# Cross-attention added to a batch: plain fp32 queries and keys, probabilities transposed in place, and the first row tile added by whole rows

## What is computed

```python
x, ctx: (32, 512, 512) fp32;  Wq, Wk, Wv: (512, 512) fp32;  16 heads of 32
q = (x @ Wq.T)  k = (ctx @ Wk.T)  v = (ctx @ Wv.T)      # split into heads
probs = softmax(q k^T / sqrt(32));  att = probs v
return x + att[0]          # the attention of batch 0, added to every batch
```

## Time and profile before

| | |
|---|---|
| median of 3 executions | 189.42 us (188.5 to 189.72) |
| the profiled execution | 188.74 us, span of its instructions 186.6 us |
| PE, DVE, ACT, POOL busy | 127.9, 105.7, 96.3, 80.7 us |
| moved by DMA | 71.52 MB, mean 383 GB/s |
| DMA issues of 256 KB, 512 KB, 1 MB | 32, 48, 32 and a few at the start |

### The profile page before, as it was taken

The page is one execution under the profiler, slowest core; times in us unless marked ns, Lnnn a source line. Parts: engine busy times, 40 slices in busy tenths (PEclk is TensorE's granted clock), DMA queues, the critical chain, the costliest instruction groups (busy, mean ns, idle before and its releaser), DMA issues.

```text
span 186.6 us, 3382 instructions
## 1 busy us (share of the span) xinstructions
PE 127.9 (69%) x1240; PEld 94.0 (50%) x1240; DVE 105.7 (57%) x171; ACT 96.3 (52%) x225; POOL 80.7 (43%) x45
## 2 busy tenths in 40 slices
PE   6999999999995978998889998798881000000000
PEld 6878877668663756775657666565550000000000
DVE  0455646643709999636699766945618999300000
ACT  2525535566476789679698778898860000000000
POOL 1000000000009999800099996399966999200000
PEclk9999999999999999999999999999999555555555
DMA  6999999999998999999999999999999999999996
GB/s 211 378 359 418 410 409 410 408 407 407 383 410 293 331 332 344 343 305 382 395 386 398 386 367 404 403 407 404 406 416 416 408 422 421 412 418 421 421 421 258
DMA packets 31968, 71.52 MB, mean 383 GB/s; under 512 B 1872, under 2 KB 10064, under 8 KB 31824
## 3 DMA queue, kind: packets, MB, share of 16 engines
q1 hardware_dynamic: 31952, 71.31, 99.9%
HBM read 37.75 MB, written 33.55 MB: 382 GB/s over the span
## 4 chain that ended last, share of the span: by engine, by line
PE 52%; DVE 14%; ACT 13%; issue 6%; DVEq 1%; POOL 0%; ACTq 0%; POOLq 0%
PE bank L387 12%; PE bank L367 8%; ACT probs L586 7%; PE bank L322 6%; PE bank L356 6%; PE bank L345 6%; DVE slots L719 5%; ACT probs_t L594 5%; PE bank L314 5%; PE bank L398 4%; DVE slots L709 3%; DVE neg_max L666 3%; PE bank L469 3%; DVE slots L702 1%; PE bank L409 1%
## 5 line engine op out<-in xcount | busy, mean ns | idle before, releaser
L272 POOL TENSOR_TENSOR slots<-slots,att_rows 128x512 f32<-128x512 f32 (+1 forms) x27 | 43.4, 1650 | 70.0 <-DVE att_rows L691 70.0
L586 ACT ACTIVATE probs<-bank,neg_max 128x512 f32<-128x512 f32 x64 | 44.9, 702 | 12.1 <-DVE neg_max L666 11.7
L666 DVE TENSOR_REDUCE neg_max<-bank 128x1 f32<-128x512 f32 x64 | 41.8, 682 | 11.9 <-PE bank L367 11.8
L387 PE MATMUL bank<-ident,probs 128*128 128x128 f32 x256 | 39.8, 281 | 7.8 <-ACT probs L586 6.7
L594 ACT COPY probs_t<-bank 128x512 f32<-128x512 f32 x64 | 37.7, 592 | 10.8 <-PE bank L387 10.0
L387 PEld LDWEIGHTS bank<-ident,probs 128*128 128x128 f32 x256 | 28.1, 140 | 21.3 <-ACT probs L586 17.1
L367 PE MATMUL bank<-k_t,x_q 32*128 32x512 f32 x192 | 24.1, 425 | 0.0
L278 POOL TENSOR_TENSOR slots<-slots,att_rows 128x1024 f32<-128x1024 f32 x8 | 18.6, 2377 | 4.8 <-DVE att_rows L691 4.8
L286 POOL TENSOR_TENSOR slots<-slots,att_rows 128x2048 f32<-128x2048 f32 x4 | 18.0, 4532 | 3.4 <-DVE att_rows L691 3.4
L702 DVE TENSOR_TENSOR slots<-slots,bank 128x512 f32<-128x512 f32 (+1 forms) x21 | 17.7, 856 | 0.1
L398 PE MATMUL bank<-probs_t,v 128*32 128x128 f32 x512 | 17.3, 276 | 0.7 <-ACT probs_t L594 0.7
(11 more groups left out here) (41 smaller groups left out, 98.6 us busy)
## 6 DMA issues: line engine op xcount, KB each, us to landing
slots<-in_x_dram SPq DMA_DIRECT2D x19, 1024.0 KB, 14.5
slots<-in_x_dram SPq DMA_DIRECT2D x26, 512.0 KB, 8.6
...
```

Of the source, the lines that this page charges most:

```text
L272: nc.gpsimd.tensor_tensor(xs, xs, a.unsqueeze(1).to_broadcast([P, BPS, a.shape[1]]), ALU.add).then_inc(added[g], 1)
L387: last = nc.tensor.transpose(bank[:, PT_BANK + h % 2, t * P:(t + 1) * P], probs[:, h % 2, t * P:(t + 1) * P], ident[:, :])
L586: nc.scalar.activation(probs[:, h % 2, :], bank[:, h % S_BANKS, :], ACT.Exp, bias=neg_max[:, h:h + 1], scale=1.0, accum_out=row_sum[:, h:h ...
L666: nc.vector.tensor_reduce(neg_max[:, h:h + 1], bank[:, h % S_BANKS, :], AX_X, ALU.max, negate=True).then_inc(max_ready, 1)
```

## The change

- Keys, queries, query weights and transposed x are plain fp32 in one piece; a query chunk and a head's scores are one matmul each. Weights of keys and values and the context stay split. Transposed x lies in the place of the raw queries, and there is one `q_t`.
- After the weights, ACT no longer empties banks: x0_t, q and q_t of row tiles 1 to 3 are copied by DVE. In `heads` of PE, turn 11 and score pair 7 go ahead of `turn_queries`.
- The probabilities of a head stay in one place: ACT writes them there, PE transposes them out of it, ACT copies the transposed ones back over it. Heads 0 to 3 of row tile 0 have places of their own in slot 15's memory, all later ones share a ring of 7. `exponent` waits until the head that had the place 7 heads ago has been weighed; it no longer waits for a transposition.
- 20 slots: groups 0 to 3 of the last half (`FRESH`) are loaded at the start. The load of slot 15 waits for the first weighing. Only groups 4 to 9 are reloaded row by row, 10 to 15 whole.
- Row tile 0 is turned back, normalised, added and stored as whole rows after all 16 heads. Three of the value chunks and the queries of row tile 1 stand later in PE's order.

The diff, without hunks that only rename units or follow from these:

```diff
@@ -29,12 +29,12 @@
     C = D // P
     HG = HEADS // HPG
     GROUPS = B // BPS
-    SLOTS = GROUPS + 1
+    SLOTS = GROUPS + 4
     PAIR = 2
     PAIRS = HEADS // PAIR
     S_BANKS = 4
     PT_BANK, BACK_BANK, ATT_T_BANK = 4, 6, 7
-    PT_SLOTS = 6
+    RING = 7
     WARM_UP = 24
     SCALE = float(DK) ** -0.5
     HI, LO = 0, 1
...
-    FIRST, SECOND, ROW_1, ROW_2, ROW_3 = 1, 2, 3, 4, 5
-    BY_ROWS, ADDED_BY_ROWS, STORED_BY_ROWS = 12, (1, 2, 3, 4, 5, 6, 7, 8), (1, 2, 3)
-    LAST_ROW_DVE_GROUPS = (4, 5, 6, 7, 8, 1, 2, 3)
...
-    FIRST_ORDER = (0, 1, 3, 2, 5, 7, 4, 9, 6, 8, 11, 10, 13, 12, 14, 15)
+    ROW_0, ROW_1, ROW_2, ROW_3 = 1, 2, 3, 4
...
+    FRESH = SLOTS - GROUPS
+    BY_ROWS = range(FRESH, FRESH + 6)
+    ADDED_BY_ROWS, STORED_BY_ROWS = (0, 1, 2, 3, 4, 5, 6, 7), (0, 1, 2)
...
...
+    FIRST_ORDER = (0, 1, 2, 3, 4, 5, 7, 6, 9, 8, 11, 10, 13, 12, 14, 15)
...
-        WQ_RAW, WK_RAW, CTX_RAW, WV_RAW, WK_T, CTX_T, WV_T = 7, 8, 9, 10, 11, 13, 15
...
+        WQ_RAW, WK_RAW, CTX_RAW, WV_RAW, WK_T, FIRST_PROBS, CTX_T, WV_T = 10, 11, 12, 13, 14, 15, 16, 18
...
-        BY_ACT = [what != "v" for what, *_ in JOBS]
-        BY_DVE = [what != "q" for what, *_ in JOBS]
+        SPLIT = ("wk_t", "ctx_t", "wv_t")
+        BY_ACT = [n <= number["wv_t", C - 1] for n in range(len(JOBS))]
+        BY_DVE = [what in SPLIT or not BY_ACT[n] for n, (what, *_) in enumerate(JOBS)]
...
         def slot_of(J, g):
-            return g if J == 0 else (g - 1) % SLOTS
...
+            return (J * GROUPS + g) % SLOTS
...
+        def place(j, h):
+            n = j * HEADS + h
+            return first_probs[:, n, :] if n < HPG else ring[:, (n - HPG) % RING, :]
+        def place_free(eng, j, h):
+            last = j * HEADS + h - RING
+            if last >= HPG:
+                eng.wait_ge(att_t_summed, last // HPG + 1)
...
-                    load(0, g)
-            sp.wait_ge(half_values_done, 1)
-            load(0, CTX_T)
-            load(0, WV_T)
+                if g == FIRST_PROBS:
+                    sp.wait_ge(att_t_summed, 1)
+                load(0, g)
             sp.wait_ge(bank_filled, number["v", T - 1] + 1)
-            load(0, CTX_T + 1)
-            load(LAST_HALF, 0)
-            LAG = 3
-            for g in FIRST_ORDER:
-                store(FIRST, g)
-            for g in range(GROUPS):
-                store(SECOND, g)
-            for g in range(1, BY_ROWS + 1):
-                reload_row(0, g)
+            for g in range(FRESH):
+                load(LAST_HALF, g)
+            LAG, ROW_LAG = 3, 10
+            for n, g in enumerate(FIRST_ORDER):
+                store(ROW_0, g)
+                if n >= ROW_LAG:
+                    reload_row(0, BY_ROWS[n - ROW_LAG])
             for g in range(GROUPS):
                 store(ROW_1, g)
-                if g >= LAG:
-                    reload(g - LAG + 1)
-            for g in range(GROUPS - LAG + 1, GROUPS):
-                reload(g)
+                if LAG - 1 <= g < GROUPS - FRESH + LAG - 1:
+                    reload(g - LAG + 1 + FRESH)
...
                     emptied(pe, "x0_t", j)
-                for a, b in PASSES:
-                    last = mm(job_bank("q", j), x0_q[:, j % 2, c, a, :], wq_t[:, c, b, :],
-                              start=(c == 0 and (a, b) == PASSES[0]), stop=(c == C - 1 and (a, b) == PASSES[-1]))
+                last = mm(job_bank("q", j), x0_t[:, c, :], wq_t[:, c, :], start=(c == 0), stop=(c == C - 1))
...
 
             def scores(j, heads_at_once):
-                for a, b in PASSES:
-                    for h in heads_at_once:
-                        g, rows = h // HPG, slice(h % HPG * DK, (h % HPG + 1) * DK)
-                        last = mm(bank[:, h % S_BANKS, :], x0_q[rows, j % 2, g, a, :], k_t[rows, g, b, :],
-                                  start=((a, b) == PASSES[0]), stop=((a, b) == PASSES[-1]))
+                for h in heads_at_once:
+                    g, rows = h // HPG, slice(h % HPG * DK, (h % HPG + 1) * DK)
+                    last = mm(bank[:, h % S_BANKS, :], q_t[rows, g, :], k_t[rows, g, :], start=True, stop=True)
                 last.then_inc(scores_ready, 1)
...
             def turn_queries(j):
-                raw_queries_out(j)
+                emptied(pe, "q", j)
...
@@ -385,7 +393,7 @@
                     pe.wait_ge(probs_t_ready, j * HEADS + h - 1)
                 for t in range(T):
                     last = nc.tensor.transpose(bank[:, PT_BANK + h % 2, t * P:(t + 1) * P],
-                                               probs[:, h % 2, t * P:(t + 1) * P], ident[:, :])
+                                               place(j, h)[:, t * P:(t + 1) * P], ident[:, :])
                 last.then_inc(transposed, 1)
 
...
                     query_chunk(j + 1, 3)
                 score_pair(j, 6)
                 if more:
-                    raw_queries_out(j + 1)
+                    emptied(pe, "q", j + 1)
                 weigh_values(j, 1)
                 turn_probs(j, 10)
+                turn_probs(j, 11)
+                score_pair(j, 7)
                 if more:
                     pe.wait_ge(att_t_ready, j * HG + 2)
                     turn_queries(j + 1)
-                turn_probs(j, 11)
-                score_pair(j, 7)
                 turn_probs(j, 12)
                 turn_probs(j, 13)
...
@@ -528,40 +536,38 @@
             value_chunk(2, 2)
             turn_probs(0, 4)
             value_chunk(2, 3)
+            turn_probs(0, 5)
             value_chunk(3, 0)
-            turn_probs(0, 5)
+            turn_probs(0, 6)
+            turn_probs(0, 7)
+            score_group(0, 2)
             value_chunk(3, 1)
             value_chunk(3, 2)
-            turn_probs(0, 6)
+            turn_probs(0, 8)
             value_chunk(3, 3)
-            turn_probs(0, 7)
-            score_group(0, 2)
-            query_chunk(1, 0)
+            turn_probs(0, 9)
             emptied(pe, "v", T - 1)
             weigh_values(0, 0)
-            query_chunk(1, 1)
-            turn_probs(0, 8)
-            query_chunk(1, 2)
-            turn_probs(0, 9)
-            query_chunk(1, 3)
+            turn_probs(0, 10)
             weigh_values(0, 1)
-            turn_probs(0, 10)
-            raw_queries_out(1)
-            turn_back(0, range(HG // 2))
             turn_probs(0, 11)
             score_group(0, 3)
-            turn_queries(1)
+            query_chunk(1, 0)
             turn_probs(0, 12)
+            query_chunk(1, 1)
             turn_probs(0, 13)
-            emptied(pe, "q_t", 1)
+            query_chunk(1, 2)
             weigh_values(0, 2)
             turn_probs(0, 14)
+            query_chunk(1, 3)
             turn_probs(0, 15)
+            turn_queries(1)
+            weigh_values(0, 3)
+            emptied(pe, "q_t", 1)
             score_group(1, 0)
-            weigh_values(0, 3)
-            turn_back(0, range(HG // 2, HG))
+            turn_back(0)
...
             def exponent(j, h):
                 act.wait_ge(max_ready, j * HEADS + h + 1)
-                if j * HEADS + h >= 2:
-                    act.wait_ge(transposed, j * HEADS + h - 1)
-                nc.scalar.activation(probs[:, h % 2, :], bank[:, h % S_BANKS, :], ACT.Exp, bias=neg_max[:, h:h + 1],
+                place_free(act, j, h)
+                nc.scalar.activation(place(j, h), bank[:, h % S_BANKS, :], ACT.Exp, bias=neg_max[:, h:h + 1],
                                      scale=1.0, accum_out=row_sum[:, h:h + 1]).then_inc(exp_ready, 1)
...
             def copy_transposed(j, h):
                 act.wait_ge(transposed, j * HEADS + h + 1)
-                before = j * HEADS + h - PT_SLOTS
-                if before >= 0:
-                    act.wait_ge(att_t_summed, before // HPG + 1)
-                nc.scalar.copy(probs_t[:, (j * HEADS + h) % PT_SLOTS, :, :],
-                               bank[:, PT_BANK + h % 2, :].rearrange("p (t n) -> p t n", t=T)).then_inc(probs_t_ready, 1)
+                nc.scalar.copy(place(j, h), bank[:, PT_BANK + h % 2, :]).then_inc(probs_t_ready, 1)
...
                         copy_transposed(j, h - 1)
-                    if j + 1 < T:
-                        if h == 2:
-                            empty("x0_t", j + 1)
-                        if h == 10:
-                            empty("q", j + 1)
-                        if h == 11:
-                            empty("q_t", j + 1)
...
-                if what == "v":
+                if what == "q":
                     dve.wait_ge(bank_filled, number[what, i] + 1)
-                    nc.vector.tensor_copy(v[:, i, :], ps).then_inc(dve_evacuated, 1)
+                    nc.vector.tensor_scalar(q_raw, ps, SCALE, None, ALU.mult).then_inc(dve_evacuated, 1)
+                elif what not in SPLIT:
+                    dve.wait_ge(bank_filled, number[what, i] + 1)
+                    if what == "q_t":
+                        dve.wait_ge(scores_ready, scores_through(i - 1, HEADS - 1))
```

(45 more changed lines are left out.)

167 lines of the change are left out of this document (75 added, 92 removed).

## The result

The changed kernel takes 197.07 us where the kernel before takes 189.25 us (medians; 195.88 to 197.53 against 188.5 to 189.72). Two more executions of the changed kernel, at 200.49 and 202.17 us, are over 1.5% above its fastest and are left out as slow. The ratio is 1.040, 95% interval 1.033 to 1.048: 4% slower. A later run of the same two kernels gave 197.6 against 189.62 us, ratio 1.041 [1.033, 1.048]. The forecast was 192.4 us with a range up to 196.3: the right direction, but more than half of the loss was missing (3.0 of 7.8 us were forecast).

What follows compares the result with a forecast made beforehand. DMA bytes and rate bound the kernel. Fourth row tile 3.5 + 1.8 + 1.7 + 0.9 = 7.9 us late, less 4.2 of slack: +3.7 on 188.74 gives 192.4 us, with DMA's end (190.4) meeting span 190.3; range 186.3 to 196.3.

Steps and rivals of the forecast that it cites:

- slack of 4.2 us: At the end of the kernel, the fourth attention row tile could be 4.2 us late before the end moves.
- 15.2 MB / 0.42 = 36.2 us: Once the first whole slot is issued at 143.55 us, storing the remaining 15.2 MB takes 36.2 us.
- Plain fp32, 0.87 per chunk and +0.17 per call: On PE, a plain fp32 matmul takes 0.87 us, +0.17 (at most +0.31) per query chunk and scores call.
- Ring, one q_t, ACT's relief: In row tile 2, waits at pair 5 and weighings 1 to 3, partly covered by ACT, lengthen 25.9 to 27.5 us.
- Row tile 0: On PE, 17.3 us of work after 47.2 plus stalls put `turn_back` at 67.5, against 66.2 now.
- Row tile 1, "3.5 us later than now": After the first `turn_back`, score pair 2 starts at 71.7; row tile 1 runs 3.5 us later than now.
- DMA: In the queue, idle times of 1.9, 5.4 and 3 us put 36.7 MB at 104, 4.2 us later; end 190.4.
- Whole rows, +4.1 us of gain: Row tile 0's 8.39 MB stored at 0.406 instead of 0.338 take 20.7 for 24.8 us, a gain of 4.1.
- 1: Rival: PE's stalls fill up, no change; `turn_back` at 64.5, fourth tile 3.7 late, time 188.1; chance 0.22.
- 2: Rival: DMA keeps its gain, queue empty for 1 us only, row tiles keep 25.8 us, time 185.5; chance 0.20.
- Rival 3: DVE or the fp32 load decides: a record costs 0.505, each tile grows by another 1.4, time 196.5; chance 0.15.
- Rival 4: 20 slots with loads still waiting for the same release: 1.9 us in the DMA sum, 0.8 to 2.5; no chance given.

Runs made afterwards that it cites:

- before_plain: The kernel before with only queries, keys, query weights and transposed x made plain fp32 in one piece: 191.18 us, ratio 1.007.
- LAG 5: The changed kernel with filled waits and, in SyncE's loop of the second row tile's stores, LAG = 5 instead of 3: 193.66 us, ratio 1.023.
- max_first: The changed kernel, nothing filled, LAG = 5, head (1,1)'s maximum taken ahead of normalizing row tile 0 on VectorE: 194.06 us, ratio 1.024.
- filled waits: The changed kernel with 9 identity transpositions in each of PE's two waits at the start of row tile 1: 195.7 us, ratio 1.029.
- the kernel with six groups by halves: The kernel before with six groups of the first row tile stored by halves, the other ten by whole rows: 193.47 us, ratio 1.026.
- act_empties: max_first with the emptying of x0_t, q and q_t for row tiles 2 and 3 back on ScalarE: 195.69 us, ratio 1.033.

## Why the prediction was wrong

Point by point, by its own steps.

- *What bounds the kernel, and the slack of 4.2 us*: right in kind. `before_plain` put the fourth `turn_back` 5.2 us back and the span only 1.9. Measured by the rule, the slack was 46.4 - 43.1 = 3.3 us; I had it 0.9 too large. The term that looks mis-sized is 15.2 MB / 0.42 = 36.2 us. When the queue is no longer behind, the same stores move at 403 GB/s (kernel with LAG 5) where before, with the queue behind, they moved at 420:

```profile
152.20:183.50 31.30, 0.00 (x0) 0.00 (x0) 16.09 (x11) 0.00 (x0) 15.57 (x4) 0.50 1.02 403
```

By 403 GB/s the term is 37.7 us, 1.5 more. That is more than the 0.9, so something else in the sum was off the other way; what, is open.

- *Plain fp32, 0.87 per chunk and +0.17 per call*: right. The chain after shows `L342 x2` at 0.86 (0.69 before) and `L376 x4` at 1.06 (0.90 before). The estimate by four passes in the Trainium skill (FP8 and Floating Point Precision, TensorE Precision Notes) was 0.93 for a chunk; the trace has 0.86, in two records.
- *Ring, one q_t, ACT's relief*: right together. Row tile 2 was forecast at 27.5 and took 27.7, the last at 23.3 and took 23.2. With plain fp32 alone (`before_plain`) they are 27.4 and 22.7, so ring, q_t and relief come to 0.3 and 0.5 us. PE's waits in row tile 2 are these, and the 0.6 before the weighing (L406) is the wait for q_t that was put at 0.75 (the weighing begins 0.1 us after DVE's copy to q_t ends):

```profile
PE bank L395 <- ACT ring L590: 1.1, 3, 0.4
PE bank L406 <- issue: 0.6, 1, 0.6
```

- *Row tile 0*: `turn_back` forecast at 67.5, measured 68.0 and, in other kernels with the same row tile 0, 66.9 and 68.1. The differences are all there at PE's first transposition of probabilities; from it to `turn_back` pass 31.2 us in each, against 30.7 before. The score pair behind it was to begin at 71.7 and begins at 72.1.
- *Row tile 1, "3.5 us later than now"*: **the step that failed.** The prediction saw the two waits (it counted PE idle from `turn_back` to the pair at 71.7) and priced them at their own length. It left out what PE's clock does behind them. There were two waits of over a microsecond within four, and the granted clock was 1.2 GHz for the next 10.2 us. Row tile 1, forecast at 29.7 us (67.5 to 97.2), took 34.3. With the waits filled it takes 30.2, so 4.1 of the 4.6 us are the clock. That all four `turn_back` of that kernel stand within 0.6 us of the forecast is in part luck, since the first came 0.6 early. With one wait fewer (`max_first`) the clock stays up as well. That these waits bring the fall about is shown by both; which of their properties does it is not.
- *DMA*: the sum had 36.7 MB done at 104 us. In the kernel with filled waits it is at 105 (349 GB/s up to there), so the gaps at 52 and at 67 to 76 us were sized to 1 us; in the changed kernel, with the fall, it is at 110. My terms also add up to 104.2, which is 4.6 us behind the 99.6 of before and not 4.2, so the DMA-bound end should have read 190.8. After 104 us I let the queue run full to the end. The landing wait of `reload_row` behind three stores, with the reloads no longer queued ahead, was not in it: about 1.5 us, taken away by LAG = 5.
- *Whole rows, +4.1 us of gain*: too large. Whole-row stores alone move 372 to 379 GB/s (the kernel with six groups by halves, 72 to 84 us and its page); 406 holds with reloads among them. 8.39 MB at 0.375 are 22.4 us, so by this estimate the gain is about 2.4 us against 24.8. The Trainium skill (DMA: Bandwidth & Descriptors, Why small descriptors are slow) gave 1.0 us by its overhead of 3 cycles for a packet; the measured figure lies between the two. In this kernel it decided nothing, because the queue had holes then.

How the terms meet, in spans: the forecast was 190.3. With both faults out (filled waits, LAG 5) it is 191.5, and 0.9 of the difference is the slack. The landing wait brings it to 193.0, the clock to 197.5. In medians the same steps are 4.7, 6.1 and 8.0 us over the kernel before beside them, where 3.0 was forecast. The clock's step is smaller in the medians, 1.9 us: the two unprofiled executions of 196.5 and 196.6 us seem to have had a shorter fall, and a late row tile also hides part of a late queue.

Of the rivals, 1 and 2 were refuted by the row tiles' lengths. Rival 3 gave nearly the right time (196.5) for a reason that isn't so: a record cost 0.43 us and not 0.505, and taking work off VectorE (`act_empties`) did not shorten row tile 1. Rival 4 is right as far as it went: the hole at 52 us is there, and is worth nothing in the kernel with LAG = 5, since closing it moves it.
